# Filling the gaps between row maxima with a matmul that nothing reads, in a two-layer transformer kernel's softmax attention

## The reference, cut to what matters

```
qkv = (x @ W_qkv.T).reshape(b, n, H, DH).transpose(0, 2, 1, 3)      # H = 16 heads of DH = 16
score = softmax(einsum('bhif,bhjf->bhij', qkv, qkv) / sqrt(DH))
attn = einsum('bhij,bhjf->bihf', score, qkv)
out = attn.reshape(b, n, F) @ W_o.T
```

## Time and profile before

| what | value |
|---|---|
| time, median of 3 runs | 3146.13 us (3145.28 to 3147.32) |
| the profiled execution's own time | 3150.74 us |
| its span, first to last instruction | 3149.0 us |
| granted TensorE clock, mean | 0.978 |
| PE busy | 3007.4 us, 96% of the span |
| DVE busy | 2435.5 us, 77% |
| ACT busy | 2055.1 us, 65% |
| softmax attention, first maximum to last | 1429.0 to 2825.1 us |

### The profile page before, as it was taken

The page is one execution under the profiler, slowest core; times in us unless marked ns, Lnnn a source line. Parts: engine busy times, 40 slices in busy tenths (PEclk is TensorE's granted clock), DMA queues, the critical chain, the costliest instruction groups (busy, mean ns, idle before and its releaser), DMA issues. The chain is left out here.

```text
span 3149.0 us, 62227 instructions
## 1 busy us (share of the span) xinstructions
PE 3007.4 (96%) x24412; PEld 1992.3 (63%) x24412; DVE 2435.5 (77%) x4822; ACT 2055.1 (65%) x3775; POOL 529.6 (17%) x608
## 2 busy tenths in 40 slices
PE   7999979997999989988999999999999999997998
PEld 6899968876899979964344333334333333344998
DVE  7533568965433589967888999999999999983987
ACT  5544535545544556642777888887888888877665
POOL 3322325543322322210000000000000000000222
PEclk9999989998999999988899999999999999999999
DMA  4211120002211100004104030200303030000000
GB/s 131 86 41 38 52 68 2 2 2 77 87 41 37 53 19 1 1 17 103 27 20 68 2 42 2 34 10 2 42 2 42 2 42 2 2 2 1 14 21 21
DMA packets 60259, 99.39 MB, mean 32 GB/s; under 512 B 7569, under 2 KB 43585, under 8 KB 57281
## 3 DMA queue, kind: packets, MB, share of 16 engines
q1 hardware_dynamic: 53632, 78.10, 11.3%
q0 software_dynamic: 6336, 17.31, 1.7%
HBM read 64.84 MB, written 30.41 MB: 30 GB/s over the span
## 5 line engine op out<-in xcount | busy, mean ns | idle before, releaser
L2386 DVE TENSOR_REDUCE smxp<-psum 128x1 f32<-128x512 f32 x2048 | 1258.6, 681 | 35.5 <-PE psum L2233 34.1
L2343 ACT ACTIVATE spr<-psum 128x512 f32<-128x512 f32 x2048 | 1114.5, 596 | 224.3 <-PE psum L2257 177.3
L2233 PE MATMUL psum<-sks,sqs 48*128 48x512 f32 x2048 | 766.8, 455 | 5.4 <-DVE spart L2378 3.0
L2257 PE MATMUL psum<-sqs,sks 50*128 50x512 f32 x2048 | 756.3, 454 | 0.0
L2274 PE MATMUL psum<-spr,sv 128*32 128x256 f32 x8192 | 660.5, 394 | 11.1 <-ACT sot L2352 8.6
L2233 PEld LDWEIGHTS psum<-sks,sqs 48*128 48x128 f32 x2048 | 313.7, 187 | 421.0 <-issue 394.9
L2274 PEld LDWEIGHTS psum<-spr,sv 128*32 128x32 f32 x8192 | 163.2, 108 | 382.2 <-ACT spr L2343 290.0
L2257 PEld LDWEIGHTS psum<-sqs,sks 50*128 50x128 f32 x2048 | 303.5, 186 | 16.4 <-issue 9.5
L1915 POOL MEMSET fhqb<- 128x64 f32 x3 | 0.3, 152 | 1490.3 <-POOLq L2143 1490.3
L547 PE MATMUL psum<-w_a,hsa_hi 128*128 (+1 forms) x1056 | 193.4, 281 | 0.9 <-DVE hsa_lo L804 0.8
L547 PE MATMUL psum<-w_b,hsb_hi 128*128 (+1 forms) x1056 | 192.6, 281 | 0.0
(11 more groups left out here) (427 smaller groups left out, 5831.4 us busy)
## 6 DMA issues: line engine op xcount, KB each, us to landing
sks<-q_parts SPq DMA_DIRECT2D x42, 256.0 KB, 9.0
sqs<-q_parts SPq DMA_DIRECT2D x42, 256.0 KB, 19.7
q_parts<-spart SPq DMA_DIRECT2D x16, 512.0 KB, 2.7
x<-in_L_attn_x_dram SPq DMA_DIRECT2D x8, 512.0 KB, 7.4
yoa<-in_L_ffn_w_dram SPq DMA_DIRECT2D x16, 256.0 KB, 2.6
xga<-f_sorted_a SPq DMA_DIRECT2D x8, 512.0 KB, 3.8
f_routed_a<-yoa SPq DMA_DIRECT2D x8, 512.0 KB, 2.9
yob<-in_L_ffn_w_dram SPq DMA_DIRECT2D x16, 256.0 KB, 2.7
```

The costliest lines, as they stand in the source:

```text
L2233: e.matmul(bank(what), QS[n % 2][rows, pr, q0:q0 + P], KS[n % 2][rows, pr, jc * GW:(jc + 1) * GW], start=True, stop=True, tile_position=(H ...
L2257: e.matmul(out, KS[n % 2][rows, pr, jt * P:(jt + 1) * P], QS[n % 2][rows, pr, ic * GW:(ic + 1) * GW], start=True, stop=True, tile_position ...
L2343: e.activation(PR[j % 2][:, HEAD[i], :], src, ACT.Exp, scale=float(DH) ** -0.5).then_inc(*done.up)
L2386: e.tensor_reduce(out[:, pr, i, jc, a:a + 1], bank(what), AX.X, ALU.max).then_inc(*pm_free[use[what] % 4].up)
```

## The change

After each maximum with a number of 64 or more, ahead of the first score, `plan()` yields one more step, `busy`. For it TensorE multiplies a 128x128 block of `PART[0]` with that buffer's 128x512 block, over all 128 rows of contraction, and writes the result into `po`. Nothing reads the result: the first product of the first unit starts its sums anew in the same bank. The step raises no semaphore. The first of the twenty waits until VectorE has written the last values that buffer gets in this stage (the third of the four late parts). No other engine has a part in the step.

```diff
                         yield ("max", m)
                         if m % 4 == 3:
                             yield from itertools.islice(late, 1)
+                        if m >= MPU:
+                            yield ("busy", m)
...
+                            if kind == "busy":
+                                if at[0] == MPU:
+                                    e.wait_ge(*read(("parts", 0, IC - 2, 1)))
+                                e.matmul(po, PART[IC % 2][:, 0, 0:P], PART[IC % 2][:, 0, :], start=True, stop=True)
```

## The result

The changed kernel takes 3163.02 us (median of 5 runs, 3159.26 to 3175.21); the one before 3145.28 us (5 runs, 3141.76 to 3147.32). Two executions far off the others, one of the kernel before (5389.09 us) and one of e4_pairs (6700.72 us), are left out of the ratios. The forecast was 3134.5 us, 3131 to 3143. The profiled execution took 3159.26 us, its span is 3157.5 us.

A forecast was written before the change was run, and what follows sets the result against it. VectorE's reduces were taken to set the pace at full clock, TensorE at half clock from 1490.8 us. Four terms of 0 and one of -11.6 us, taken from the median 3146.13 us, gave 3134.5 us, range 3131 to 3143.

The forecast's parts named there:

- What it adds on TensorE: Twenty matmuls 0.23 us apart, hidden under VectorE's 0.60 us per maximum: cost 0, upper bound 6.7 us at half clock.
- The clock holds: With the added matmuls the clock stays at 1.00 through 1477 us and after 1485 us; chance 0.66.
- The same picture: One full-height matmul beside every maximum was likened to 1431 to 1459 us: 46 value records for 48 maxima, clock 1.00.
- Rival A: Clock goes down and up in turns while the added matmuls run; gain 9.3 us, 3136.8 us; chance 0.08.
- The gain of 11.6 us: With the clock held, 26 reduces from 1490.83 us take 16.2 instead of 27.75 us; bounds 11.2 and 12.0.
- Rival B: The half-clock stretch is shorter in timed runs than in the profiled one; gain 7.0 us, 3139.1 us; chance 0.10.
- The sum: Whole kernel: 0 + 0 + 0 + 0 - 11.6 us, giving 3134.5 us from the median.
- Queue: Maxima from 64 on, behind the first added matmuls, do not hold VectorE up: cost 0, at most 0.2 us.
- wait: First added matmul waits for VectorE's third late part, done at 1470.5 us with 2.9 us to spare: cost 0.
- first score: The first score, at 1485.38 us right behind maximum 84, does not move: cost 0.
- Rival C: Nothing changes: the clock still falls at about 1477 us; 3146 us; chance 0.08.
- rival D: The fall is put off to the first key tile, then 41 us at half clock; 5.9 us slower, 3152.0 us; chance 0.08.

The follow-up runs named there:

- e4_pairs: The change with its twenty full-height matmuls placed two in a row after every second maximum; 3140.18 us against 3142.42 before, ratio 0.9989; timed again, 0.9994.
- e6_double: The change with two full-height added matmuls behind every maximum, forty in all; 3158.52 us against 3155.18 for the kernel before, ratio 1.0017.
- e1_half: The change with added matmuls of 64 rows, in the row half the maximum leaves free; 3144.74 us against 3142.42 before, ratio 1.0000.
- e7_halves: The change with two added 64-row matmuls, one in each row half, behind every maximum; median 3152.66 us against 3155.18 before, ratio 0.9988.
- e5_short: The change with added matmuls of 128 columns instead of 512; 3166.07 us against 3155.18 for the kernel before, ratio 1.0038.
- e3_values: The change with one value-projection copy after every fourth maximum, five in all, replacing the twenty matmuls; median 3141.20 us, ratio 1.0005 to the kernel before.

## Why the prediction was wrong, step by step

**What it adds on TensorE: cost 0. Wrong, and the first of two failures.** The step took a spacing of 0.23 us from rows where every matmul is of one kind and used it for two kinds in alternation. Measured: 0.43 us each at full clock, 0.72 at half; 0.86 and 1.45 us per maximum instead of 0.47 and 0.93. The upper bound of 6.7 us was therefore no bound: maximum 64 to 84 grew by 13.0 us. e4_pairs and e6_double (like behind like at 0.23 us), e1_half and e7_halves (no change of kind) and e5_short (a shorter stream) show that the alternation is the cause of this cost. No row that the prediction rested on has the two kinds in turn, one by one, so the cost should have been given as unknown, with a load and a stream for each as its upper end. The trace before did hold a warning, in the place that the prediction took as its picture, where values (L2221, full height) are followed by a maximum (loads, PEld):

```profile
1447.02 0.73 PEld L2221 LDWEIGHTS psum<-wqkv1T,sao 128*128 128x128 f32 x4 [0.41 <-DVE smxp L2386]
1448.08 0.32 PEld L2233 LDWEIGHTS psum<-sks,sqs 48*128 48x128 f32 x2 [0.33 <-issue]
```

Four loads of the values stand close together, and then none runs for 0.33 us before that of the maximum. There it happens once in four maxima.

**The clock holds: wrong, the second failure.** It fell at 1474.4 us in the changed kernel's profile, 4.6 us after maximum 64, with PE busy 4.00 of 4 us. "The same picture" as 1431 to 1459 us was a count of records; how they stand in time was another matter. Rival A had a fall under the added matmuls, but with the clock back for half of them, and not the price. That added work can hold the clock is right: with the same matmuls in pairs it was 1.00. What in the alternation brings it down stays open: it fell in e1_half without one and stayed up in e6_double with one on either side of every maximum. The lower clock then made each alternation dearer, 1.45 instead of 0.86 us. Of the 13.0 us the twenty maxima would have lost some 5 at full clock, by calculation (20 x 0.86 = 17.2 against 12.5; no run kept the clock with this order); the other 8 are the half clock's. The fall came earlier and ended earlier as well, at 1508.5 us, which gave 8.0 us back between maximum 84 and 128.

The Trainium skill, "TensorE: Matmul & The Clock Gate", section "Part 3: Packing small matmuls — row/col tiling", says that a weight load is pulled ahead of running matmuls where it targets other rows, or the second weight buffer. e1_half agrees with the first half (both start at 1474.88 us). For the second the traces are divided: full height behind full height is covered, 0.23 us apart, full height behind half height is not, 0.43.

**The gain of 11.6 us: right in the profile, mis-sized for the median of the timed runs.** Where the clock held, 84 to 128 took 28.0 to 28.1 us against 39.3, so 11.2 to 11.3 us: the term is right to 0.4 us against a profiled execution. But the median run of before doesn't lose that much. Against it e4_pairs gains 2.2 and 1.0 us, e7_halves 2.5. Rival B said this (a shorter stretch at half clock in the timed runs), but not that it was this strong: the forecast's base, the median less the full term, could not have come out even with a held clock. The runs' clock is the only trace of it: 0.981 against 0.985 with the clock held is about 0.004 x 3149 x 2 = 25 us at half clock in a timed run, by that rounded figure, where the profiles have 41 to 44. The first 13.6 of them would lie under VectorE's pace, and the rest would cost 11.4 x (1 - 1.24 / 2.16) = 4.9 us, still more than measured, so this accounts for a part only. The single runs show more than the median: of the 34 runs of before beside e4_pairs, 13 have a mean clock of 0.976 to 0.979 and a median of 3149.14 us, the other 21 have 0.980 to 0.983 and 3140.84 us. Against the 13 e4_pairs gains 9.0 us, near the term, against the 21 it gains 0.7. The three profiled executions of before belong with the 13. A run's mean clock doesn't say where its half clock lay, so that the 13 had theirs in this place is likely and not shown. Whether taking a profile lengthens the half clock or the three happened to be of that sort is open; no run here separates it.

**The sum, anew.** Maximum 64 to 128 takes 56.8 us in both profiles of the change and 40.5 with the clock held (e3_values, e4_pairs). The median run of before stands 1 to 2 us above the latter by e4_pairs, 2.5 by e7_halves, and 4.3 by e6_double (48.1 us for this stretch, and 3.3 us slower than before), so at some 42 to 45. The change is then 12 to 15 us slower, 1.0038 to 1.0048 by ratio, where the two groups of runs measured 1.0062 (1.0045 to 1.0079) and 1.0043 (1.0027 to 1.0060). The first group's centre lies above that, and what it adds was not found.

**Queue, wait, first score.** Nothing came of the wait on the parts. The first score did move, by 13.7 us (25.94 against 12.25 us after maximum 64), because maximum 84 did. **Rival C** (nothing changes) and **rival D** (the fall put off) did not come true in the change. D's mechanism exists: e7_halves fell at 1504.1 us, in its first key tiles. Its price of 5.9 us did not show there: the half clock lasted 30.7 us, not the 41 that D took, and 84 to 128 took 39.3 us as before.

## What to carry to other kernels

A spacing read between matmuls of one kind does not hold between two kinds: look for a place in the trace where exactly the two alternate, and take at least one load and one stream each if there is none. If filler work must go among row-tiled matmuls, put it in runs behind a pair of them, or give it the same tiling; over the twenty maxima the same twenty matmuls cost 13 us in the profile in one order and nothing in another. And before a term is taken off the median of the runs, compare the granted clock of the timed runs with that of the profiled one, and look at the single runs: what a half-clock stretch costs in the profile may not be there to be won in the median run.

## What the runs showed of the hardware that was not expected

- A matmul on 48 of the array's rows followed by one on 128 rows, and the reverse, costs 0.43 us at 512 columns and full clock, 0.72 at half, with a load of 0.19 (0.29) us that nothing covers. Two of 128 rows follow each other at 0.23 us.
- A matmul busy share of 100% did not keep the clock: in the changed kernel it fell with PE busy 4.00 of 4 us, and stayed at 0.50 through 34.1 us in which PE had no gap. PE busy 8.00 of 8 us with paired matmuls kept 1.00.
- Executions of one program differ in their mean clock, and their times with it: e3_values had 0.978 to 0.986 and 3133.75 to 3154.49 us over twelve runs, the kernel before 0.976 to 0.983 and 3135.76 to 3155.21 us over 34.
